# Two of five chunks of attention probabilities turned by VectorE and sixteen SBUF-to-SBUF transfers in place of TensorE

## The reference, cut to what matters

```python
q = _rope(_rmsnorm(q, q_norm_w), pos)              # 8 batches, 128 tokens, 32 heads of 128
k = _rope(_rmsnorm(k, k_norm_w), pos)              # 8 key heads of 128
k_all = jnp.concatenate([kc, k], axis=1)           # 512 cached keys and 128 new ones
v_all = jnp.concatenate([vc, v], axis=1)
scores = jnp.einsum('bqhd,bkhd->bhqk', q, k_all) * SCALE
scores = jnp.where(valid[:, None, None, :], scores, -1e+30)
probs = jax.nn.softmax(scores, axis=-1)
o = jnp.einsum('bhqk,bkhd->bqhd', probs, v_all)
x = x + jnp.einsum('bse,de->bsd', o, Wo)
```

## Time and profile before

| | |
|---|---|
| median of 3 runs | 1352.56 us |
| profiled execution, span from first to last instruction | 1349.8 us |
| time around the span (median less span) | 2.8 us |
| TensorE busy | 1342.4 us, 99% |
| VectorE busy | 1040.8 us, 77% |
| ScalarE busy | 843.2 us, 62% |
| GpSimd busy | 713.6 us, 53% |
| transposes of probabilities on TensorE (line 1131) | 1280, between 29.6 and 1080.1 us |

### The profile page before, as it was taken

How to read it: one execution, slowest core, us unless ns; L and a number is a source line. 1 busy time by engine, 2 the same in 40 slices (tenths; PEclk the granted TensorE clock), 3 DMA queues, 4 the chain that set the end, 5 groups by cost and what they waited for, 6 DMA issues and landing times.

```text
span 1349.8 us, 24930 instructions
## 1 busy us (share of the span) xinstructions
PE 1342.4 (99%) x7812; PEld 1191.3 (88%) x7812; DVE 1040.8 (77%) x2131; ACT 843.2 (62%) x2217; POOL 713.6 (53%) x972
## 2 busy tenths in 40 slices
PE   9999999999999999999999999999999999999999
PEld 8888888888889998889888989888888888888887
DVE  7988777877787778777877787778778887748546
ACT  7676566666566556666666666566665785545444
POOL 7767465646554655565555555555555652305111
PEclk9999999999999999999999999999999999999999
DMA  5566325522552264126413641364222164354532
GB/s 201 172 185 198 87 82 173 145 63 78 187 127 59 78 201 134 38 84 206 130 31 108 203 109 31 113 210 128 79 48 48 63 191 140 125 183 141 187 141 78
DMA packets 170746, 168.11 MB, mean 125 GB/s; under 512 B 129856, under 2 KB 137664, under 8 KB 159936
## 3 DMA queue, kind: packets, MB, share of 16 engines
q1 hardware_dynamic: 164928, 131.21, 33.3%
q0 software_dynamic: 5760, 36.18, 8.1%
HBM read 133.81 MB, written 33.55 MB: 124 GB/s over the span
## 4 chain that ended last, share of the span: by engine, by line
PE 98%; POOL 1%; DVE 1%; ACT 1%; issue 0%; POOLq 0%; DVEq 0%
PE ps L64 27%; PE ps L63 27%; PE ps L65 27%; PE ps L1131 10%; PE ps L1109 2%; PE ps L1153 1%; PE ps L2038 1%; PE ps L1103 1%; PE ps L2071 0%; PE ps L2070 0%; PE ps L2024 0%; PE ps L2023 0%; PE ps L1332 0%; DVE at_scores L897 0%; PE ps L2009 0%; ACT at_mask L601 0%
## 5 line engine op out<-in xcount | busy, mean ns | idle before, releaser
L502 POOL TENSOR_SCALAR at_probs<-at_probs,at_row_inv 128x640 f32<-128x640 f32 x256 | 211.8, 828 | 151.1 <-DVE at_row_inv L903 150.9
L605 ACT ACTIVATE at_pT_hi<-ps 128x512 fp32r<-128x512 f32 x320 | 186.5, 604 | 101.1 <-PE ps L65 50.9
L897 DVE CUSTOM_DVE_ANT_0 at_scores<-ps,at_mask,at_inv_rms 128x640 f32<-128x640 f32 x256 | 220.2, 879 | 31.7 <-PE ps L65 30.8
L653 ACT ACTIVATE at_probs<-at_scores,at_neg_max 128x640 f32<-128x640 f32 x256 | 211.9, 836 | 51.0 <-DVE at_neg_max L897 51.0
L845 DVE TENSOR_TENSOR at_pT_lo<-ps,at_pT_hi 128x512 fp32r<-128x512 f32 x320 | 212.6, 686 | 25.7 <-ACT at_pT_hi L605 20.7
L63 PE MATMUL ps<-ds_hi,x_hi 128*128 128x512 f32 (+1 forms) x564 | 192.7, 342 | 0.0
L65 PE MATMUL ps<-ds_hi,x_lo 128*128 128x512 f32 (+1 forms) x564 | 192.0, 340 | 0.0
L648 ACT ACTIVATE at_square<-ps 128x128 bf16<-128x128 f32 x256 | 67.1, 276 | 166.7 <-DVE a_raw L876 149.9
L1131 PE MATMUL ps<-ident,at_probs 128*128 128x128 f32 x1280 | 160.6, 273 | 0.0
L63 PE MATMUL ps<-at_kT_hi,ds_lo 128*128 128x320 f32 x512 | 158.1, 309 | 1.6 <-DVE at_neg_max L897 1.6
L65 PE MATMUL ps<-at_kT_hi,ds_lo 128*128 128x320 f32 x512 | 158.2, 309 | 0.0
(11 more groups left out here) (215 smaller groups left out, 3379.6 us busy)
## 6 DMA issues: line engine op xcount, KB each, us to landing
kT_pages<-shared SPq DMA_DIRECT2D x16, 1024.0 KB
kv_raw<-kT_pages SPq DMA_DIRECT2D x60, 256.0 KB, 4.0
v_pages<-shared SPq DMA_DIRECT2D x14, 1024.0 KB
kv_raw<-v_pages SPq DMA_DIRECT2D x56, 256.0 KB, 4.1
sw_wgu_raw<-in_sw_gu SPq DMA_DIRECT2D x22, 512.0 KB, 3.3
staging<-in_L_cond_Wo SPq DMA_DIRECT2D x8, 1024.0 KB, 4.8
staging<-in_L_cond_Wq SPq DMA_DIRECT2D x7, 1024.0 KB
sw_b_raw<-in_sw_bgu SPq DMA_DIRECT2D x88, 64.0 KB, 2.8
```

The source lines that it names most:

```text
L502: pool.tensor_scalar(probs[:, h, :], probs[:, h, :], row_inv[:, h:h + 1], 1.0, ALU.mult, ALU.mult).then_inc(probs_done, 1)
L605: act.activation(out, src, ACT.Copy).then_inc(done, 1)
L653: act.activation(probs[:, h, :], scores[h % 2][:], ACT.Exp, bias=neg_max[:, h:h + 1], scale=-1.0, accum_out=row_sum[:, h:h + 1]).then_inc( ...
L897: dve.tensor_tensor_reduce(out=scores[h % 2][:], in0=slot(h), in1=mask[:, b, :], scale=inv_rms[b % 2][:, h:h + 1], scalar=3.0e38, op0=ALU. ...
```

## The change

For 62 of the 64 steps (`by_moves`: all but the first and the last) chunks 3 and 4 are no longer turned by TensorE.

- VectorE turns 32 x 32 squares: `turn_squares` for each head, 128 partitions x 256 elements, four a step, into `turned`. Two stand ahead of `attended`, one behind the last `inverse`, one behind `cached_keys`.
- That leaves each 32 x 32 square turned but in the wrong partition block. `move_turned` copies the blocks to their places in `pT_raw`: 16 transfers of 32 partitions x 256 elements (32 KB) a step, eight issued by SyncE and eight by ScalarE, each half behind a wait for all four heads of `turned_done`. Both stand first in a step on their engine; on ScalarE that is ahead of `pT_hi` 0.
- `pT_hi` and `pT_lo` 3 and 4 read `pT_raw` in SBUF, not PSUM. On ScalarE they move behind `exps` 0 and 1, on VectorE behind `inverse` 0 and 1.
- TensorE issues `score` 2 and 3 ahead of `times_v` 3 and 4; `score` 1 waits for three chunks only.
- VectorE's `mask_and_max` 3 and ScalarE's `exps` 2 move ahead of `attended` and `oT_hi`. GpSimd's `stage_pages` moves ahead of two residuals and `rotate_q`. Some semaphores are merged and the scratch for GpSimd's own transfers is halved, to make room.

```diff
+        turned = sb("turned", [P, NQ, MOVED, G, SQ])
+        pT_raw = sb("pT_raw", [P, NQ, MOVED, G, SQ])
...
+            def move_turned(g, b):
+
+                wait_apart(sp, turned_done, upto(g, b, G), passed)
+                for a in range(NQ // 2):
+                    for k in range(NQ):
+                        sp.dma_start(pT_raw[k * SQ:(k + 1) * SQ, a], turned[a * SQ:(a + 1) * SQ, k]).then_inc(pT_moved[b % 2], 16)
...
             def group(g, last):
                 for b in range(B):
                     g2, b2 = following(*following(g, b))
+                    if by_moves(g, b):
+                        move_turned(g, b)
...
+            def move_turned(g, b):
+
+                act.wait_ge(turned_done, upto(g, b, G))
+                for a in range(NQ // 2, NQ):
+                    for k in range(NQ):
+                        act.dma_start(pT_raw[k * SQ:(k + 1) * SQ, a], turned[a * SQ:(a + 1) * SQ, k]).then_inc(pT_moved[b % 2], 16)
...
+                    if by_moves(g, b):
+                        move_turned(g, b)
                     probs_T(g, b, 0)
                     probs_T(g, b, 1)
...
+            def turn_squares(g, b, h):
+
+                wait_apart(dve, probs_done, upto(g, b, G, h + 1), passed)
+                dve.transpose(turned[:, :, :, h, :].rearrange("p k c r -> p c k r"),
+                              probs[:, h, (KC - MOVED) * P:KEYS].rearrange("p (c k i) -> p c k i", c=MOVED, k=NQ)).then_inc(turned_done, 1)
...
-                    for c in range(2, KC):
+                    for c in range(2, KC - MOVED if by_moves(g, b) else KC):
                         probs_T(g, b, c)
...
-                        pe.wait_ge(pT_done, upto(g, b, KC, KC))
+                        pe.wait_ge(pT_done, upto(g, b, KC, KC - MOVED if by_moves(g, b) else KC))
...
                     times_v(g, b, 2)
+                    if by_moves(g, b):
                         score(g1, b1, 2)
                         score(g1, b1, 3)
+                        times_v(g, b, 3)
+                        times_v(g, b, 4)
```

## The result

The changed kernel takes 1876.7 us (median of 4 runs, 1876.03 to 1879.95) against 1352.64 us on the same chip: a ratio of 1.388, 95% interval 1.386 to 1.390. That is 39% slower, 524 us. The direction was forecast; the time lies above the range.

What follows compares the result with a forecast made beforehand. TensorE, busy 99%, was taken to set the pace. Per step -0.85 (transposes) + 3.3 (head) + 1.5 (middle) = +3.95 us, times 62 = +245 us, giving 1595 us, 18% slower; range 1375 to 1725.

Steps and rivals of the forecast that it cites:

- What is removed: TensorE's eight transposes a step, 0.106 us each: 0.85 us a step, 52 us over 62 steps, all on the path.
- When ScalarE begins: Step's head: the fourth turn (0.41 us) ends at about T, the start of `probs_T` 0; ScalarE's issues begin then.
- The price of an issue: Step's head: 0.47 us per ScalarE transfer, 3.76 us for eight before `at_pT_hi` 0; TensorE stalls 3.3 us a step.
- The upper bound of 0.94: Most per ScalarE issue, 2 x 0.47 us, if the two engines issuing at once take turns at one generator.
- The clock: Rival: TensorE's clock falls to its lower level; 3 us a step would be +186 us, 1783; chance 0.04.
- The middle: After `project_q`: TensorE stalls 0.45 us at `times_v` 3, 0.85 at `times_v` 4, 0.2 after `project_kv`; 1.5 us a step.
- What costs nothing: Two other turns, landing (6 us of cover; otherwise stall at `times_v` 3), SyncE's loads, 0.5 MB more, GpSimd's reordering: no cost.
- the free issue: Rival: issuing costs ScalarE next to nothing, only the middle is left; +0.65 us a step, 1393 us; chance 0.16.
- The shared generator: Rival: ScalarE and SyncE share one generator; at 0.80 us an issue, 2.6 us more a step, about 1760; chance 0.15.

Runs made afterwards that it cites:

- The run with the short normalisation: Changed kernel without transfers (1490.6 us), with GpSimd's normalisation of head 0 cut from 640 to 128 elements: 1460.9 us.
- two experiments: Changed kernel with ScalarE's eight issues moved behind its third high part: 1620.1 us; changed kernel with all sixteen transfers issued by SyncE: 1659.1 us.
- the first experiment: Changed kernel with SyncE starting its eight transfers only after ScalarE's first high part, so the two no longer issue together: 1872.1 us.

## Why the prediction was wrong in size

It said +3.95 us a step, and a plain step shows +7.63. By its own steps:

- **What is removed**, -0.85 us of TensorE's work: right as work, but it is not all gain. The claim "all on the path" fails by 0.2 to 0.4 us a step in the runs without transfers.
- **When ScalarE begins**: "about T"; the fourth turn ended at T - 0.08. The turn, 0.41 us by interpolation, measured 0.44.
- **The price of an issue: the first failed step.** I took 0.47 us from the earlier trace rows. Measured 5.02 / 8 = 0.63, with a median row of 0.61. Those rows are loads from DRAM, and in the changed kernel SyncE's loads of keys still take 0.39 (its loads of values, issued right behind them, 1.32 in the median). A transfer from SBUF to SBUF costs ScalarE 0.56 to 0.61 at the three sizes tried, and also alone; why it costs more than those rows no run shows. The upper bound of 0.94 held it; the value taken did not. It is 1.3 of the 3.68 us missed.
- **The clock: the second.** It stood as a rival of 0.04, apart from the forecast, though the forecast itself left TensorE standing for 3.3 us a step. The two belonged together: the level is down after 4.65 us, and after waits of 1.8 to 2.4 us (by the brackets) it is down or up, even within one run. I also priced it high (186 us; 107 measured). It is 1.53 us of the miss.
- **The middle: the third.** Forecast 0.45 + 0.85 + 0.2 = 1.5 us, measured 2.30: 1.05 before `times_v` 3, 0.67 before `times_v` 4, 0.2 before `output`, and 0.1 for each restart. The failed sentence is that a residual from SBUF takes 0.68 us like one from PSUM. That holds for chunk 4 (0.67 us at 819.80), which starts ahead of GpSimd's pass, and not for chunk 3 (1.19 us at 817.80), which starts behind the one at 817.66. The run with the short normalisation gave 30 us back.
- **What costs nothing**: the landing was hidden, as said, and "if it went, the stall would move to `times_v` 3" is what two experiments show. GpSimd's reordering may be free, but its normalisation was not; nor was the turns' place in VectorE's program.
- **Longer steps**, with weights or with a lower clock that lasts longer, were taken as plain ones: 51 us.

Of the rivals, the free issue is out: the chain has 16% on ScalarE's queue. With it falls, for this kernel, the sentence of the Trainium skill (DMA: Bandwidth & Descriptors, Issuing engines are not separate DMA queues) that the sequencer's time is usually small beside the transfer: it is 5.0 us a step on the path. The shared generator is out as a mechanism by the first experiment; its price per issue, 0.80 us, was as far above the measured 0.63 as my 0.47 was below. The lock that the Trainium skill (Perfetto Trace Analysis, DMA Instruction — HWDGE) describes does not show here: ScalarE's median row is 612 ns with SyncE issuing at the same time, and 612 ns without.

## What to carry to other kernels

An issue is an instruction of its engine: count the issues, price them from a row of the same kind (memory to memory), and put them where that engine would be idle, never in front of what the busiest engine waits for. When a forecast contains a standstill of a few microseconds on TensorE, price the slower restart with it rather than beside it as a rival. And before taking work off an engine that is 99% busy, see what the next ones would need to be early: here the whole saving was 52 us, and without any transfer at all, in the order of before, the other engines let through 2.

## What the hardware showed that I had not expected

- SBUF to SBUF transfers cost ScalarE 0.61 us each and SyncE 0.59 to 0.60 for 16 or 32 KB, and 0.53 (SyncE) to 0.56 us (ScalarE) for 128 KB over 128 partitions. Loads from DRAM of 256 KB take SyncE 0.39 us (keys) and 1.32 us (values, right behind) in the median of the changed kernel:

```profile
L353 SPq DMA_DIRECT2D kv_raw<-kT_pages x60: 378/389/553, 81.4 to 1558.2; - x60
L359 SPq DMA_DIRECT2D kv_raw<-v_pages x56: 929/1322/5561, 183.0 to 1558.8; - x56
```

- VectorE's 128x512 subtraction takes 1.19 us in place of 0.67 with both sources in SBUF when it starts behind GpSimd's pass over SBUF, and 0.76 when that pass is cut to 128 elements. When VectorE starts first, GpSimd's pass takes 1.06 us in place of 0.80.
- After 4.65 us without work TensorE ran 3.5 us at a granted clock of 0.52; in 13 of 60 steps it ran about 6 us at the lower level. After waits of 1.8 to 2.4 us both outcomes are seen, so what decides between them is open.
- With the turns in its program VectorE pauses 1.7 to 3.2 us at the start of the second to sixth pass of the loop with nothing in the profile to wait for; without them it does not. The cause is open.
